# One-hot matrices stored tile by tile, with their 128 positions adjacent, in a transformer block with expert choice

## The chip, the cores and the metric

The kernel runs on one core of a Trainium2 chip. The metric is device time in microseconds of one launch. The core has TensorE (PE in the rows; its weight loads, which overlap matmuls, are PEld), VectorE (DVE), ScalarE (ACT), GpSimd (POOL) and SyncE (SP), which issues transfers. Each runs its own instructions in order and waits on semaphores for the others.

## The reference

x is 16 x 256 rows of 256 values, N = 4096 rows. First cross-attention, then a feed-forward layer in which each of 8 experts picks its 1024 best rows:

```
x = x + _L0_xattn_ref(_layernorm(x), ctx, ctx, Wq, bq, Wk, bk, Wv, bv)
x = x + _L0_ffn_ref(_layernorm(x), Wg, W1, b1, W2, b2)
# _L0_ffn_ref:
S = jax.nn.sigmoid(xt @ Wg).T            # 8 x 4096
G, I = jax.lax.top_k(S, k)               # k = 1024
ex = xt[I]
hid = jax.nn.gelu(einsum('ekh,ehf->ekf', ex, W1) + b1, approximate=False)
out = (einsum('ekf,efh->ekh', hid, W2) + b2) * G[..., None]
new_x = jnp.zeros_like(xt).at[I.reshape(-1)].add(out.reshape(-1, h))
```

## The kernel before

Rows are held as 32 tiles of 128 (NT = 32, P = 128), row t*128+p on partition p. The attention half (up to about 141 us) works through groups of four tiles. Products are made of 16-bit high and low parts, three matmuls for one (helper `pairs`, L1026). In its course the router's matmuls (L1120, four per tile: 128 weight columns from x2T, 16 moving columns from wg16) give the logits. A search on VectorE then finds each expert's threshold (to about 173 us), and two prefix products give each chosen row its place from 0 to 1023 in the expert's list; rows not chosen get a place out of reach. `split_places` cuts a place into loi (its low 7 bits, the position in a tile of the list) and hii (the tile of the list, 0 to 7).

The list of an expert is then made as a product. VectorE's `places(e)` copies the expert's column of loi to lo_e (L896, bf16) and of hii to hi_e, compares the latter with 0 to 7 (inhi) and writes val: for each tile t, inhi times the tile's number and inhi times the partition's number, 16 columns. `onehot` (L907), called four times (HOTS = 4), compares lo_e with the constants 0 to 127 in iota16, which GpSimd wrote once near the start (L407). The result oneh is 1 where row t*128+p has position k. TensorE's `list_of(e)` (L1257) adds up 32 matmuls, one per tile t, with oneh of that tile as weights (128 x 128) and val of that tile as the moving side (128 x 16). What comes out is the tile number and the partition number of the row at each place of the list. VectorE copies it out (idp, L915) and makes the row numbers (ids, L922); GpSimd gathers the rows with 8 indirect transfers (L447) into ex, SyncE turns them with DMA transposes (L287) into exT; for the first expert's first four tiles TensorE transposes (L1295) and ScalarE and VectorE (L1012) copy.

`expert(e)` on TensorE is 16 units of six matmuls with 512 columns (first layer; ScalarE applies gelu to each, L594 and L598, VectorE takes the low part, L967), then 8 tiles of 24 matmuls with 256 columns (second layer; VectorE L981, ScalarE L611, GpSimd scatters with addition, L460). Expert 0 is written out, experts 1 to 5 are a loop on every engine, 6 and 7 are written out. Lists are made ahead: list 0 before any expert, list 1 behind the first unit of expert 0 (SPLIT = 1), list e+2 behind the second layer of expert e. The one-hots of list e+2 are made by VectorE in the second layer of expert e, one call each in its tiles 3 to 6, `places` in its tile 0; those of lists 0 and 1 in one piece. The order on each engine is the order in which the code is written; semaphores named in `then_inc` and `wait_ge` join them: lo_s, val_s and hot_s (VectorE to TensorE), id_mm (back), const3 (the iota).

Of the kernel before, what the change touches and what calls it, by code (L numbers as in the profile page):

```python
# [26 lines left out]
BF16 = mybir.dt.bfloat16  # L27
# [5 lines left out]
P = 128  # L33


def build(nc, x_d, ctx_d, wq_d, bq_d, wk_d, bk_d, wv_d, bv_d, wg_d, w1_d, b1_d, w2_d, b2_d, out_d):
# [4 lines left out]
    NT = N // P  # L41
# [5 lines left out]
    KT = K // P  # L47
# [14 lines left out]
    HOTS = 4  # L62
# [6 lines left out]
    with ExitStack() as stack:  # L69
        def sb(name, shape, dt=F32):  # L70
            return stack.enter_context(nc.sbuf_tensor(name, shape, dt))

        def sem(name):
            return stack.enter_context(nc.semaphore(name))
# [9 lines left out]
        onesf = sb("onesf", [P, P])  # L84
        pick = sb("pick", [P, E])
        order16 = sb("order16", [P, 4, P], BF16)
        iota16 = sb("iota16", [P, P, NT], BF16)
        iota8 = sb("iota8", [P, NT, KT])
        tileno = sb("tileno", [P, NT, KT])
        partno = sb("partno", [P, 1])  # L90
# [61 lines left out]
        pos = sb("pos", [P, NT, E], I32)  # L152
        loi = sb("loi", [P, NT, E], I32); hii = sb("hii", [P, NT, E], I32)

        lo_e = sb("lo_e", [P, NT], BF16)
        hi_e = sb("hi_e", [P, NT])
        oneh = sb("oneh", [P, P, NT], BF16)
        inhi = sb("inhi", [P, NT, KT])
        val = sb("val", [P, NT, 2, KT], BF16)
        idp = sb("idp", [P, 2, KT])  # L160
# [44 lines left out]
        s = {n: sem(n) for n in names}  # L205
# [102 lines left out]
        def _(pool):  # L308
# [83 lines left out]
            def normed_rows(m):  # L392
# [6 lines left out]
                for t in range(TP):  # L399
# [4 lines left out]

            pool.wait_ge(s["const1"], 5)
            ln1_scale(0)
            pool.iota(iota16[:], [[1, P], [0, NT]], base=0, channel_multiplier=0,  # L407
                      allow_small_or_imprecise_dtypes=True).then_inc(s["const3"], 1)
            ln1_scale(1)
            pool.wait_ge(s["ld_bv"], 16)  # L410
# [216 lines left out]
        def _(dve):  # L627
# [264 lines left out]
            def places(e, first):  # L892

                if not first:
                    dve.wait_ge(s["id_mm"], e)
                dve.tensor_copy(lo_e[:], loi[:, :, bass.ds(e, 1)].rearrange("p t o -> p (t o)")).then_inc(s["lo_s"], 1)  # L896
                dve.tensor_copy(hi_e[:], hii[:, :, bass.ds(e, 1)].rearrange("p t o -> p (t o)")).then_inc(s["hie_s"], 1)
                dve.wait_ge(s["hie_s"], e + 1)
                dve.tensor_tensor(inhi[:], iota8[:], hi_e[:, :].unsqueeze(2).broadcast_to([P, NT, KT]), ALU.is_equal).then_inc(s["hi_s"], 1)
                dve.wait_ge(s["hi_s"], e + 1)  # L900
                dve.tensor_tensor(val[:, :, 0, :], inhi[:], tileno[:], ALU.mult).then_inc(s["val_s"], 1)
                dve.tensor_scalar(val[:, :, 1, :], inhi[:], partno[:, 0:1], None, ALU.mult).then_inc(s["val_s"], 1)
                dve.wait_ge(s["lo_s"], e + 1)

            def onehot(k0, k1):

                dve.tensor_tensor(oneh[:, k0:k1, :], iota16[:, k0:k1, :], lo_e[:, :].unsqueeze(1).broadcast_to([P, k1 - k0, NT]),  # L907
                                  ALU.is_equal).then_inc(s["hot_s"], 1)

            def read_list(e, first, from_=D_):  # L910
# [28 lines left out]
            def b1_of(e, first):  # L939
                if not first:  # L940
                    dve.wait_ge(s["h_hi"], 2 * FC * e)
                dve.tensor_copy(b1e[:], bcol[:, bass.ds(e * FC, FC)]).then_inc(s["b1e_s"], 1)
# [13 lines left out]
            def expert(e, first, next1, next2):  # L956


                b1_of(e, first)
                if not first and next1:  # L960
                    read_list(e + 1, False, D_)
                for u in range(2 * FC):
                    h, f = u // FC, u % FC
                    if first and u == SPLIT:
                        read_list(1, False, C_)
                    dve.wait_ge(s["h_hi"], 2 * FC * e + u + 1)
                    dve.tensor_tensor(hid[1][:, f, h * 512:(h + 1) * 512], g32[:, u % 2, :], hid[0][:, f, h * 512:(h + 1) * 512],  # L967
                                      ALU.subtract).then_inc(s["h_lo"], 1)
                    if u % 2 and u // 2 < 4:
                        w2_split(e, u // 2, first)  # L970
                    if u == KEEP:
                        keep(e, first)
                        if next1:
                            ids_of(e + 1, False)
                for t in range(KT):
                    dve.wait_ge(s["y_mm"], KT * e + t + 1)
                    if t == 0:
                        dve.wait_ge(s["b2e_s"], e + 1)
                    if not (first and t < 2):
                        dve.wait_ge(s["y_o"], KT * e + t - 1)  # L980
                    dve.scalar_tensor_tensor(yt[:, t % 2, :], C_[:, t % 2, 0:D], 1.0 / FS, b2e[:],  # L981
                                             ALU.mult, ALU.add).then_inc(s["y_t"], 1)
                    if next1 and t < 4:
                        w1_lo(e + 1, t)
                    if next2:
                        if t == 0:
                            places(e + 2, False)
                        elif t >= KT - 1 - HOTS:
                            if t < KT - 1:
                                j = t - (KT - 1 - HOTS)  # L990
                                onehot(P // HOTS * j, P // HOTS * (j + 1))

            def onehots():
                for j in range(HOTS):
                    onehot(P // HOTS * j, P // HOTS * (j + 1))

            dve.wait_ge(s["const2"], 5)
            places(0, True)
            dve.wait_ge(s["const3"], 1)
            onehots()  # L1000
# [20 lines left out]
        def _(pe):  # L1021
# [31 lines left out]
            for i in range(2):  # L1053
                for c in range(DC):
                    for e in range(DC):
                        last = pe.transpose(B_[:, i, e * D + c * P:e * D + (c + 1) * P], w_raw[:, i, c, e * P:(e + 1) * P], ident[:])
# [9 lines left out]
            for d in range(DC):  # L1066
                last = pairs(A_[:, 0, d * D:(d + 1) * D], lambda a, e: wkT[a][:, e, d * P:(d + 1) * P],
                             lambda b, e: wqcT[b][:, e, :], DC)
            last.then_inc(s["m_mm"], 1)
            pe.wait_ge(s["b_col"], 1)  # L1070
            for d in range(DC):
                for e in range(DC):
                    last = pe.matmul(A_[:, 1, P + d:P + d + 1], wqc[:, e, d * P:(d + 1) * P], bcol[:, NB1 + DC + e:NB1 + DC + e + 1],
                                     start=e == 0, stop=e == DC - 1)
# [145 lines left out]
            for h in range(2):  # L1220
                last = pe.transpose(A_[:, 0, h * P:(h + 1) * P], logit[:, h * HT:(h + 1) * HT, :].rearrange("p t e -> p (t e)"), ident[:])
# [28 lines left out]
            def list_of(e, first, to=D_):  # L1250

                pe.wait_ge(s["val_s"], 2 * (e + 1))
                if not first:
                    pe.wait_ge(s["id_ev"], e)
                pe.wait_ge(s["hot_s"], HOTS * (e + 1))
                for t in range(NT):
                    last = pe.matmul(to[:, 0, 0:2 * KT], oneh[:, :, t], val[:, t].rearrange("p a j -> p (a j)"),  # L1257
                                     start=t == 0, stop=t == NT - 1)
                last.then_inc(s["id_mm"], 1)

# [31 lines left out]
            for t in range(KT // 2):  # L1292
                pe.wait_ge(s[f"gat_{t}"], 16)
                for c in range(4):
                    last = pe.transpose(rowT16[t][:, c * P:(c + 1) * P], ex16[:, t, c * P:(c + 1) * P], ident16[:])  # L1295
# [27 lines left out]
```

## Time and profile before

| | us |
|---|---|
| median of 3 runs | 547.64 (547.56 to 548.38) |
| the profiled execution | 549.17 |
| its span, first to last instruction | 547.4 |
| TensorE busy | 491.1 (90%) |
| VectorE busy | 332.0 (61%) |
| ScalarE busy | 307.8 (56%) |
| GpSimd busy | 293.2 (54%) |
| mean granted TensorE clock, of its full speed | 0.944 |

The rows below have the time from the start of the span first, in us. "xN" counts instructions. A merged row's duration goes from its first start to its last end. What stands in brackets is idle time of the engine ahead of the row and what ended it. Busy time of TensorE is no measure of its use, since matmuls overlap: the distance of the starts is. PEclk is the granted clock as a share of 2.4 GHz; 0.50 is the level of 1.2 GHz.

### The profile page before, as it was taken

What the parts mean: (1) busy time and instruction counts of PE and PEld (TensorE: products, weight loads), DVE (VectorE), ACT (ScalarE), POOL (GpSimd) and SP (SyncE); (2) the same over time, 40 slices, a digit from 0 to 9 for tenths busy, and PEclk for the clock granted to TensorE, in tenths of its full rate; (3) what the DMA queues carried; (4) which work ended last, traced back from release to release, by engine and by line L of the source; (5) the groups of instructions that cost most, each with busy time, mean ns of one, the idle gap of its engine ahead of it and who ended that gap; (6) DMA issues with size and microseconds to landing.
All of it is one profiled execution on the core that took longest, in us unless ns stands there. A gap on an engine that the chain in (4) does not pass through costs nothing.

```text
span 547.4 us, 10408 instructions
## 1 busy us (share of the span) xinstructions
PE 491.1 (90%) x3671; PEld 351.6 (64%) x3671; DVE 332.0 (61%) x739; ACT 307.8 (56%) x562; POOL 293.2 (54%) x436
## 2 busy tenths in 40 slices
PE   4999999998523299999999999999999999999995
PEld 3777777777411245864874884794685586486484
DVE  7477777876588847547538538546645654733720
ACT  3666666654534059249439519727826925935921
POOL 5736998893600416734653671671672763555055
PEclk9999999998655589999999999999999999999998
DMA  7312555545195155943862771771782593484024
GB/s 237 107 46 69 153 147 134 137 131 150 38 275 157 41 130 172 171 72 127 141 121 76 156 144 27 200 149 19 195 162 29 152 180 55 136 126 49 0 31 50
DMA packets 91929, 64.19 MB, mean 117 GB/s; under 512 B 53044, under 2 KB 87800, under 8 KB 91896
## 3 DMA queue, kind: packets, MB, share of 16 engines
q1 hardware_dynamic: 79248, 46.42, 31.1%
q0 software_dynamic: 12288, 17.05, 18.8%
q8 instruction: 19, 0.31, 0.2%
q10 hardware_dynamic: 360, 0.30, 0.2%
q14 instruction: 14, 0.11, 0.1%
HBM read 35.83 MB, written 16.91 MB: 96 GB/s over the span
## 4 chain that ended last, share of the span: by engine, by line
PE 59%; issue 6%; DVE 5%; POOL 4%; DMA 2%; SPq 2%; ACT 1%; POOLq 0%; DVEq 0%; ACTq 0%
PE bank L1026 54%; PE bank L1257 3%; POOL out L460 2%; DVE junk L794 2%; SPq L266 2%; POOL xrow L387 1%; DMA out<-yo,ids_s 1%; DMA rows_d<-xrow 1%; POOL ex L447 1%; DVE thr L815 1%; PE bank L1233 1%; DMA ex<-rows_d,ids 1%; DMA yo<-xrow 0%; DVE oneh L907 0%; POOL xrow L379 0%
## 5 line engine op out<-in xcount | busy, mean ns | idle before, releaser
L1026 PE MATMUL bank<-w2h,xres 128*128 128x256 f16 x1024 | 169.0, 273 | 0.0
L1026 PE MATMUL bank<-exT,w1h 128*128 128x512 f16 x512 | 153.3, 381 | 0.6 <-DVE exT L1012 0.6
L1026 PE MATMUL bank<-w2l,xres 128*128 128x256 f16 x512 | 139.7, 273 | 0.0
L967 DVE TENSOR_TENSOR xres<-g,xres 128x512 f16<-128x512 f32 x128 | 87.6, 690 | 60.4 <-ACT xres L598 60.4
L460 POOL DMA_INDIRECT out<-yo,ids_s x64 | 101.0, 1577 | 25.6 <-issue 24.9
L1026 PEld LDWEIGHTS bank<-w2h,xres 128*128 128x128 f16 x1024 | 100.1, 98 | 12.5
L594 ACT ACTIVATE g<-bank,b1e 128x512 f32<-128x512 f32 x128 | 88.0, 688 | 25.4 <-PE bank L1026 20.3
L611 ACT ACTIVATE yo<-yt,ge 128x256 f32<-128x256 f32 x64 | 32.5, 508 | 119.5 <-DVE yt L981 119.5
L1026 PE MATMUL bank<-exT,w1l 128*128 128x512 f16 x256 | 97.7, 381 | 0.0
L1026 PEld LDWEIGHTS bank<-exT,w1h 128*128 128x128 f16 x512 | 49.8, 98 | 59.5 <-issue 1.4
L598 ACT ACTIVATE xres<-bank,b1e 128x512 f16<-128x512 f32 x128 | 87.2, 681 | 0.0
L981 DVE SCALAR_TENSOR_TENSOR yt<-bank,b2e 128x256 f32<-128x256 f32 x64 | 27.2, 425 | 88.6 <-PE bank L1026 87.9
L447 POOL DMA_INDIRECT ex<-rows_d,ids x64 | 65.4, 1021 | 19.6 <-issue 19.5
L445 POOL TENSOR_TENSOR pool_tick<-eps 128x1 f32<-128x1 f32 x8 | 4.7, 586 | 107.7 <-DVE ids L922 107.7
L1026 PEld LDWEIGHTS bank<-w2l,xres 128*128 128x128 f16 x512 | 50.0, 98 | 6.7
L459 POOL TENSOR_TENSOR pool_tick<-eps 128x1 f32<-128x1 f32 x64 | 15.4, 241 | 55.9 <-ACT yo L611 34.5
L1026 PEld LDWEIGHTS bank<-exT,w1l 128*128 128x128 f16 x256 | 25.1, 98 | 30.6 <-issue 0.6
L400 POOL TENSOR_SCALAR xn<-xres,st,rstd 128x256 f32<-128x256 f32 x24 | 29.0, 1219 | 0.6
L953 DVE SCALAR_TENSOR_TENSOR w2l<-w2r,w2h 128x512 f16<-128x512 f32 x32 | 22.1, 692 | 1.1
L371 POOL TENSOR_TENSOR xres<-xres,bv_bc 128x1024 f32<-128x1024 f32 x8 | 18.8, 2351 | 6.8 <-ACT xn L487 6.8
L643 DVE SCALAR_TENSOR_TENSOR w1l<-w1r,w1h 128x512 f16<-128x512 f32 x32 | 21.7, 682 | 0.0
L907 DVE TENSOR_TENSOR oneh<-iota,lo_e 128x1024 bf16<-128x1024 bf16 x32 | 21.4, 684 | 0.0
(215 smaller groups left out, 779.7 us busy)
## 6 DMA issues: line engine op xcount, KB each, us to landing
w1r<-in_L_ffn_W SPq DMA_DIRECT2D x8, 1024.0 KB, 6.6
w2r<-in_L_ffn_W SPq DMA_DIRECT2D x8, 1024.0 KB, 5.3
ctx<-in_ctx SPq DMA_DIRECT2D x8, 512.0 KB, 5.0
xres<-in_x SPq DMA_DIRECT2D x8, 512.0 KB, 5.9
rows_d<-xrow SPq DMA_DIRECT2D x8, 512.0 KB, 3.5
out<-xres SPq DMA_DIRECT2D x4, 1024.0 KB, 9.1
b_bc<-in_L_ffn_b SPq DMA_DIRECT2D x8, 128.0 KB, 4.5
ex<-rows_d,ids POOLq DMA_INDIRECT x64, 3.8
```

The costliest lines, as they stand in the source:

```text
L400: pool.tensor_scalar(xn2[:, m % 2, t], xres[:, m * TP + t], st2[:, t // 2, 1 + 3 * (t % 2):2 + 3 * (t % 2)], rstd2[:, t:t + 1], ALU.subtra ...
L447: pool.indirect_dma_start(out=ex[:, t, :], out_offset=None, in_=rows_d, in_offset=bass.IndirectOffsetOnAxis(ap=ids[:, t:t + 1], axis=0)).t ...
L460: pool.indirect_dma_start(out=rows_out, out_offset=bass.IndirectOffsetOnAxis(ap=ids_s[:, t:t + 1], axis=0), in_=yo[:, t, :], in_offset=Non ...
L594: act.activation(g32[:, u % 2, :], src, ACT.Gelu, bias=b1e[:, f:f + 1], scale=1.0 / (XS * FS))
L598: act.activation(hid[0][:, f, h * 512:(h + 1) * 512], src, ACT.Gelu, bias=b1e[:, f:f + 1], scale=1.0 / (XS * FS)).then_inc(s["h_hi"], 1)
L611: act.activation(yo[:, t, :], yt[:, t % 2, :], ACT.Copy, scale=ge[:, t:t + 1]).then_inc(s["y_o"], 1)
L643: dve.scalar_tensor_tensor(w1[1][:, c, cols], w1r[:, c, cols], FS, w1[0][:, c, cols], ALU.mult, ALU.subtract).then_inc(s["w1_lo_s"], 1)
L907: dve.tensor_tensor(oneh[:, k0:k1, :], iota16[:, k0:k1, :], lo_e[:, :].unsqueeze(1).broadcast_to([P, k1 - k0, NT]), ALU.is_equal).then_inc ...
L953: dve.scalar_tensor_tensor(w2[1][:, rows], w2r[:, rows], FS, w2[0][:, rows], ALU.mult, ALU.subtract).then_inc(s["w2_lo_s"], 1)
L967: dve.tensor_tensor(hid[1][:, f, h * 512:(h + 1) * 512], g32[:, u % 2, :], hid[0][:, f, h * 512:(h + 1) * 512], ALU.subtract).then_inc(s[" ...
L981: dve.scalar_tensor_tensor(yt[:, t % 2, :], C_[:, t % 2, 0:D], 1.0 / FS, b2e[:], ALU.mult, ALU.add).then_inc(s["y_t"], 1)
L1026: last = pe.matmul(out, lhs(a, c), rhs(b, c), start=i == 0, stop=i == len(terms) - 1)
```

## The change

oneh is stored as [partition, tile, position] and no more as [partition, position, tile], so that one tile's 128 weight columns are adjacent, where they were 32 elements apart. A call of `onehot` makes all 128 positions of 8 tiles and no longer 32 positions of all 32 tiles; it writes one run of 1024 elements. For that iota16 shrinks from 128 x 32 to 128 elements per partition and is read once per tile. lo_e holds each row's position twice, side by side, and is read in pairs, 64 times over for a tile.

```
-        iota16 = sb("iota16", [P, P, NT], BF16)
+        iota16 = sb("iota16", [P, P], BF16)
-        lo_e = sb("lo_e", [P, NT], BF16)
+        lo_e = sb("lo_e", [P, NT, 2], BF16)
-        oneh = sb("oneh", [P, P, NT], BF16)
+        oneh = sb("oneh", [P, NT, P], BF16)
...
-            pool.iota(iota16[:], [[1, P], [0, NT]], base=0, channel_multiplier=0,
+            pool.iota(iota16[:], [[1, P]], base=0, channel_multiplier=0,
...
-                dve.tensor_copy(lo_e[:], loi[:, :, bass.ds(e, 1)].rearrange("p t o -> p (t o)")).then_inc(s["lo_s"], 1)
+                dve.tensor_copy(lo_e[:], loi[:, :, bass.ds(e, 1)].broadcast_to([P, NT, 2])).then_inc(s["lo_s"], 1)
...
-            def onehot(k0, k1):
-
-                dve.tensor_tensor(oneh[:, k0:k1, :], iota16[:, k0:k1, :], lo_e[:, :].unsqueeze(1).broadcast_to([P, k1 - k0, NT]),
+            def onehot(j):
+
+                part = slice(NT // HOTS * j, NT // HOTS * (j + 1))
+                dve.tensor_tensor(oneh[:, part].rearrange("p t (k o) -> p t k o", o=2),
+                                  iota16[:].rearrange("p (k o) -> p k o", o=2).unsqueeze(1).broadcast_to([P, NT // HOTS, P // 2, 2]),
+                                  lo_e[:, part].unsqueeze(2).broadcast_to([P, NT // HOTS, P // 2, 2]),
                                   ALU.is_equal).then_inc(s["hot_s"], 1)
...
-                                onehot(P // HOTS * j, P // HOTS * (j + 1))
+                                onehot(j)
...
-                    last = pe.matmul(to[:, 0, 0:2 * KT], oneh[:, :, t], val[:, t].rearrange("p a j -> p (a j)"),
+                    last = pe.matmul(to[:, 0, 0:2 * KT], oneh[:, t], val[:, t].rearrange("p a j -> p (a j)"),
```

Every engine has the same number of instructions in the same order as before, and the same waits. VectorE's sequence ahead of the first list, with the tiles of the words above, shows the one size that differs there:

```order
 L884 TENSOR_SCALAR hii<-pos 128x32
-L896 CAST lo_e<-loi 128x32
+L896 CAST lo_e<-loi 128x64
 L897 CAST hi_e<-hii 128x32
 L899 TENSOR_TENSOR inhi<-iota,hi_e 128x256
 L901 TENSOR_TENSOR val<-inhi,tileno 128x32x8
 L902 TENSOR_SCALAR val<-inhi,partno 128x32x8
```

Nothing moved there; the cast writes twice as many elements.

## Rows read from the trace of the kernel before

**Rows 1.** Page, part 4: shares of the chain that ended last, by line

```profile
PE bank L1026 54%; PE bank L1257 3%; POOL out L460 2%; DVE junk L794 2%; SPq L266 2%; POOL xrow L387 1%; DMA out<-yo,ids_s 1%; DMA rows_d<-xrow 1%; POOL ex L447 1%; DVE thr L815 1%; PE bank L1233 1%; DMA ex<-rows_d,ids 1%; DMA yo<-xrow 0%; DVE oneh L907 0%; POOL xrow L379 0%
```

**Rows 2.** Chain in order of time, the experts: start, duration (us), work

```profile
237.77 1.93 PE bank L1257 x32
239.71 41.70 PE bank L1026 x288
...
455.92 1.78 PE bank L1257 x32
```

**Rows 3.** Instructions in order of time around list 0

```profile
180.79 2.02 PE L1257 MATMUL bank<-val,oneh 128*128 128x16 bf16 x32 [5.02 <-DVE oneh L907]
182.85 0.17 DVE L915 COPY idp<-bank 128x16 f32<-128x16 f32 x1 [0.40 <-PE bank L1257]
```

**Rows 4.** Weight loads of both kinds; min/median/max ns; L1120 in order of time

```profile
L1257 PEld LDWEIGHTS bank<-val,oneh x256: 137/167/191, 180.8 to 457.4; 128*128 128x128 bf16 x128
L1120 PEld LDWEIGHTS bank<-wg,yo x96: 94/96/100, 63.3 to 134.1; 128*128 128x128 f16 x96
133.73 0.56 PE L1120 MATMUL bank<-wg,yo 128*128 128x16 f16 x16 [0.81 <-DMA yo<-xrow]
134.14 0.27 PE L1026 MATMUL bank<-vh,pTh 128*128 128x256 f16 x1
```

**Rows 5.** L1257 in stretches: length, PE busy, PEld busy, PEclk, DMA share, GB/s

```profile
180.00:184.00 4.00, 2.02 (x32) 1.95 (x32) 0.50 0.01 4
...
455.00:459.00 4.00, 1.94 (x32) 1.96 (x32) 1.00 0.50 62
```

**Rows 6.** TensorE around list 1, in order of time; a stretch with PEclk (0.57)

```profile
194.90 0.63 PE L1026 MATMUL bank<-exT,w1l 128*128 128x512 f16 x1
195.32 2.05 PE L1257 MATMUL bank<-val,oneh 128*128 128x16 bf16 x32
197.23 0.59 PE L1026 MATMUL bank<-exT,w1h 128*128 128x512 f16 x2
...
197.66 0.38 PE L1026 MATMUL bank<-exT,w1l 128*128 128x512 f16 x1
...
195.50:196.00 0.50, 0.50 (x13) 0.50 (x11) 0.00 (x0) 0.35 (x1) 0.00 (x0) 0.57 0.58 194
```

**Rows 7.** Instructions in order of time ahead of expert 0

```profile
186.95 2.53 DVE L907 TENSOR_TENSOR oneh<-iota,lo_e 128x1024 bf16<-128x1024 bf16 x4
...
192.24 0.42 DVE L1012 COPY exT<-bank 128x512 f16<-128x512 f16 x1 [2.43 <-PE bank L1295]
```

**Rows 8.** VectorE's groups: shapes, count, busy us, mean ns of one, idle before

```profile
L907 DVE TENSOR_TENSOR oneh<-iota,lo_e 128x1024 bf16<-128x1024 bf16 x32 | 21.4, 684 | 0.0
L635 DVE TENSOR_TENSOR vl<-bank,vh 128x1024 f16<-128x1024 f32 x7 | 8.6, 1225 | 11.0 <-ACT vh L507 11.0
L635 DVE TENSOR_TENSOR vl<-bank,vh 128x512 f16<-128x512 f32 x2 | 1.3, 687 | 0.0
```

**Rows 9.** VectorE at a turn of the loop, in order of time

```profile
412.29 0.42 DVE L981 SCALAR_TENSOR_TENSOR yt<-bank,b2e 128x256 f32<-128x256 f32 x1 [1.60 <-PE bank L1026]
412.87 0.17 DVE L942 COPY b1e<-bcol 128x8 f32 x1 [0.15 <-issue]
```

**Rows 10.** GpSimd and ScalarE near the start, in order of time

```profile
14.45 4.18 POOL L407 IOTA iota<- 128x4096 bf16 x1
...
23.94 2.06 ACT L487 ACTIVATE xn<-xres,nmr,rstd 128x256 f32<-128x256 f32 x4
```

**Rows 11.** ScalarE in the last first layer, catching up after a wait

```profile
511.30 0.69 ACT L594 ACTIVATE g<-bank,b1e 128x512 f32<-128x512 f32 x1 [0.24 <-DVE xres L967]
...
512.45 0.69 ACT L594 ACTIVATE g<-bank,b1e 128x512 f32<-128x512 f32 x1
```

**Rows 12.** SyncE's four transposes for expert 0, and TensorE, in order of time

```profile
196.54 5.13 SPq L287 DMA_TRANSPOSE exT<-ex  x4
...
206.29 0.60 PE L1026 MATMUL bank<-exT,w1h 128*128 128x512 f16 x2
```

More of the change, by code:

```diff
@@ L990, in expert @@
                                 j = t - (KT - 1 - HOTS)
-                                onehot(P // HOTS * j, P // HOTS * (j + 1))
+                                onehot(j)
             def onehots():
                 for j in range(HOTS):
-                    onehot(P // HOTS * j, P // HOTS * (j + 1))
+                    onehot(j)
             dve.wait_ge(s["const2"], 5)
```

## Prediction

> **What bounds the kernel now.** I read the shares of the chain that ended last first. Matmuls of the helper at L1026 hold 54% of it, and the 256 list matmuls of L1257 3% [rows 1]. Then the chain in order of time [rows 2]: lists and expert matmuls take turns back to back, 237.77 + 1.93 is where the 41.70 us of expert matmuls begin, and the same again up to the last list at 455.92 and the expert matmuls behind it. So TensorE's own sequence sets the expert half, and a list stands bare in it: nothing runs on TensorE beside it. The first list (180.79) is also bare, but for another reason: TensorE had waited for the one-hots, and VectorE waits for its end [rows 3], GpSimd's gathers behind it.
>
> What does a list matmul take? It has 128 weight columns and 16 moving columns, as a router matmul at L1120 has [rows 4]. Their weight loads last 167 and 96 ns. Durations overlap, so the pace counts. Sixteen router matmuls start at 133.73 and the next work starts at 134.14: 0.41 us, 25.6 ns each [rows 4]. The list of 237.77 takes 1.93 us on the chain, 60 ns each, the fastest, of 455.92, 1.78, 56 ns [rows 2]. Between the two kinds three things differ: the router reads each weight column next to the last one and in f16, in groups of four; the list steps 32 elements (64 bytes) from one weight column to the next, in bf16, in one group of 32. The step is what the change removes. That it is the step is supported by the first list: TensorE's clock was granted at 0.50 there, its 1.2 GHz level, and its 2.02 us, less some 0.2 for the last one, over 31 still give 59 ns, the pace of the full clock [rows 3, 5]. A column or issue limit of TensorE itself would have doubled, as a 512-column matmul does: one from 194.90 to 195.32, 0.42 us, before the clock rose, two from 197.23 to 197.66, 0.215 each, after [rows 6]. A limit outside of TensorE's clock, the reading of the weights, does not.
>
> **The change, part by part.**
>
> *Six lists at the full clock (237.8 to 455.9).* Now 11.43 us together, the first 1.93 and the last 1.78 [rows 2]. At the router's pace 32 matmuls take 32 x 0.0256 = 0.82 us, six of them 4.9. Gain **6.5 us**. The bound from below is a pace that holds for 16 only, from above nothing better than 25.6 is in the trace.
>
> *The first list, at half clock.* No contiguous run of small matmuls stands in the trace at 1.2 GHz. Bounds: the pace is not TensorE's (25.6 ns, 31 x 0.0256 + 0.2 = 0.99 us, gain 1.0) or it is and doubles (51 ns, 1.78 us, gain 0.25). I take the second, since everything else on TensorE doubled [rows 6].
>
> *The second list.* It starts at 195.32 at half clock; the 195.5 to 196 slice has a mean of 0.57, so the clock rose near 195.93, while TensorE was at work [rows 6]. It now takes 195.32 to 197.23 = 1.91. After, it starts 0.22 earlier, 195.10; until 195.93 16 matmuls pass at 51 ns, the other 16 take 0.41: 1.24 us, gain 0.67; with 25.6 ns all through 0.82, gain 1.1.
>
> *The one-hots on VectorE.* Four operations of 1024 elements before and after. Now 684 ns each for 1024 bf16 elements, where 1024 elements at L635 take 1225 ns and 512 take 687: two elements per cycle [rows 8]. The new form reads lo_e in runs of two (its double), iota16 in rows of 128 and writes one run of 1024. No row has runs of two. Bounds: 684 ns (no cost), or 1225 ns, one per cycle, +0.54 each. I take 684, because the innermost pair is adjacent in all three tensors, which is all that the operation had of lo_e's pairs before. The cover, if not: in the expert loop VectorE idles 1.60 us ahead of a tile of the second layer [rows 9], enough for 0.54; before the second list the one-hots end at 189.48 and the exT copy that releases TensorE waits to 192.24, 2.76 us later, enough for 4 x 0.54 = 2.2 [rows 7]. Before the first list there is none: they end where TensorE's 5.02 us of waiting ends [rows 3], +2.2 us.
> A rule of the Trainium skill bears on this (Vector Engine (DVE) Microarchitecture Reference, section 5.1, Performance modes): two results per cycle need 16-bit types, an innermost step of 1 and more than one element innermost, and rows of two were measured to keep the mode. By that rule the cost is 0, as I took it; no run here shows a row of two yet.
>
> *lo_e.* One cast of 64 in place of 32 elements; L635's slope is (1225 - 687)/512 = 1.05 ns per element [rows 8], so +0.03 us. It is bare once, before the first list [rows 3]; in the loop it lies in VectorE's idle time, and before the second list in the 2.76 us.
>
> *iota16 on GpSimd.* The 4.18 us of L407 (14.45 to 18.63) shrink by a factor of up to 32. Behind it on GpSimd stand the scale of the second four tiles and add_bv. ScalarE takes the scale up at 23.94, 5.3 us behind the iota and with no idle time ahead of that row, so it wasn't what it waited for [rows 10]. Gain at the end: 0, and that GpSimd is earlier by 4 us there delays nothing.
>
> *What a shorter list uncovers.* ScalarE needs 511.30 to 512.45 = 1.15 us for a unit when it catches up, TensorE 1.295 (6 matmuls), so ScalarE doesn't become the bound [rows 11]. The second half of the first expert's rows is turned by four transposes, the last issue ending at 201.67; TensorE reads them from 206.29 [rows 12]. That is 4.6 us, less a flight that no row shows here; the second list eats 0.7 to 1.1 of it; gathers and transposes move with the first list. Each later expert's gather starts from ids made inside the expert, so all of it moves together. At a turn of the loop TensorE's sequencer has the list's time to pass the branch: 1.9 us now, 0.8 then. VectorE's own turn costs at most from 412.29 to 412.87, 0.58 us [rows 9], so I cost it at nothing.
>
> **Sum.** 6.5 + 0.25 + 0.67 - 0.03 = 7.4 us. Against its own execution, 549.17 us with a span of 547.4, that is 541.8 and 540.0. The median of the runs, 547.64, lies 1.5 below that execution; the forecast is 547.64 - 7.4 = **540.2 us**. With the half-clock pace at 25.6 ns the sum is 6.5 + 1.0 + 1.1 = 8.6: 539.0.
>
> **The rivals.**
> *The pace does not last.* Rows show it for 16 in a row only, behind long matmuls that let instructions pile up. If matmuls 17 to 32 go at 57 ns, each full-clock list loses 16 x 0.031 = 0.5 us, six 3.1: 543.3. If instead the branch takes more than 0.8 us, four turns lose up to 1.1 each, 4.4: 544.6. Against: no gap behind any list now, and VectorE's 0.58.
> *One-hots at one element per cycle:* -2.2 of the gain: 542.4.
> *The clock rises later.* TensorE worked from 192.6 or so, when the exT copy had ended, to 195.93, 3.3 us, at half clock [rows 6, 7]; as much again would cost half of it, 1.6: 541.8. Against: the dense work starts earlier and stays as dense.
> *The step isn't it.* The pace stays 56 to 61 ns, from bf16 or the long group: 547.6. Against: the half-clock list above, and that groups of four on the same columns run at 25 ns with no break between them.
> The Trainium skill has a rule on this side (TensorE: Matmul & The Clock Gate, Weight-path perf modes): fast weight load reads 128 columns of a non-FP32 type, packed or strided, up to a step of 1,024 elements. By it a step of 32 is loaded fast already and the time stays 547.6; the 167 against 96 ns speak against it.
> *Slower:* the one-hot costs more than one cycle per element for its runs of two. Its place is VectorE before both lists. An extra x on each costs 4x at the first and, past the cover, 4x - 2.76 at the second; 8x - 2.76 exceeds 7.4 from x = 1.27 us, an operation of 1.95. At two cycles per element (2 x 1.07 + 0.15 = 2.29, x = 1.6) it is 10.0 - 7.4 = 2.6 slower: 550.2. The longest 1024 elements of two sources on VectorE in my rows take 1225 ns [rows 8].
>
> **How the numbers follow.** Forecast 0.70; pace doesn't last 0.10; one-hots at one per cycle 0.07; clock later 0.03; step isn't it 0.06; slower 0.04. The range takes the forecast's two ends, 539.0 and 540.2, with 0.2 for the spread of runs, and goes up over 541.8 and 542.4 to 543.3: 538.8 to 543.4, about 0.85. What a measurement can tell from no change is about 0.2%, 1.1 us. Faster by more: 0.70 + 0.10 + 0.07 + 0.03 = 0.90; within: 0.06; slower: 0.04.
>
> **What would show it.** List matmuls at a pace near 25 ns and weight loads near 96; stretches between expert matmuls of 0.8 us in place of 1.9; the first list's duration tells 25 from 50 ns at half clock; one-hots at 684 ns; no idle time of TensorE at the turns; the half-clock stretch ending at 195.9 or so; the iota at 0.2 us with nothing else moved by it. Wrong would be: a list at 1.9 us, an idle TensorE behind a list, or exT transposes waited for at the second half of the first expert.

## The result, and the profile after

| | before | after |
|---|---|---|
| median of the runs on the same chip, us | 548.01 (547.56 to 549.37, 4 runs) | 540.66 (539.06 to 541.63, 4 runs) |
| the profiled execution, us | 549.17 | 540.94 |
| its span, us | 547.4 | 539.2 |
| mean granted TensorE clock | 0.944 | 0.943 |

The ratio is 0.9859, with a 95% interval of 0.9828 to 0.9889. On a second chip it was 0.9848 (0.9833 to 0.9863), with 539.85 us. Forecast were 540.2 us and a range of 538.8 to 543.4.

The page of the kernel after, its parts 1 and 4. PE is busy for 483.1 us, 491.1 before. In part 4 the list matmuls are L1260 now, the expert matmuls L1029:

```profile
span 539.2 us, 10408 instructions
...
PE 483.1 (90%) x3671; PEld 343.1 (64%) x3671; DVE 331.4 (61%) x739; ACT 308.2 (57%) x562; POOL 290.6 (54%) x436
...
PE bank L1029 55%; POOL out L460 2%; DVE junk L794 2%; SPq L266 2%; PE bank L1260 1%; POOL xrow L387 1%; DMA out<-yo,ids_s 1%; DMA rows_d<-xrow 1%; POOL ex L447 1%; DVE thr L815 1%; PE bank L1236 1%; DMA ex<-rows_d,ids 1%; DMA yo<-xrow 0%; DVE oneh L908 0%; POOL xrow L379 0%
```

The lists' share of the chain went from 3% [rows 1] to 1%, and nothing else rose by more than a point. The chain of waits in order of time, after (start, duration, work):

```profile
235.29 0.79 PE bank L1260 x32
236.08 41.70 PE bank L1029 x288
277.78 0.79 PE bank L1260 x32
278.57 0.12 issue
278.69 41.85 PE bank L1029 x288
320.54 0.79 PE bank L1260 x32
```

Against [rows 2]: a list holds 0.79 us where it held 1.93, and the 288 expert matmuls behind it hold 41.70 as before. What is new is the 0.12 of "issue" (time in which the engine waited for nothing that the profile shows) and 41.85 in place of 41.70 where a turn of the loop lies: that is looked at below. The instructions behind these rows, by the tile oneh (min/median/max ns, first and last start) and by line and shape (busy us, mean ns, idle before):

```profile
L1260 PEld LDWEIGHTS bank<-val,oneh x256: 95/96/151, 179.7 to 449.3; 128*128 128x128 bf16 x128
...
L908 DVE TENSOR_TENSOR oneh<-iota,lo_e 128x1024 bf16<-128x1024 bf16 x32 | 21.4, 684 | 0.0
```

A weight load lasts 96 ns, the router's number [rows 4], where it lasted 167; a one-hot still 684 ns [rows 8].

Where the 8.2 us between the two profiled spans lie, from the starts of matched instructions in the two traces:

| stretch | before | after | difference | forecast |
|---|---|---|---|---|
| start of the span to list 0's first matmul | 180.79 | 179.72 | 1.07 | -0.03 |
| list 0's first matmul to expert 0's first | 12.02 | 11.48 | 0.54 | 0.25 |
| expert 0's first matmul to the one behind list 1 | 4.42 | 3.41 | 1.01 | 0.67 |
| from there to list 2 | 40.38 | 40.51 | -0.13 | 0 |
| list 2 to the end of the span | 309.8 | 304.1 | 5.74 | 6.5 |

Without the first row this is 7.16 us, against a forecast of 7.4. Of the 5.74, the six lists from their start to the next expert matmul give 5.71: 11.55 us before, 5.84 after.

These are distances in one execution of each kernel. In the profiled execution of the same changed kernel on the second chip the last four differences are 0.49, 1.01, -0.85 and 5.73, together 6.4: there TensorE's clock rose 5.2 us behind expert 0's first matmul, and in the execution of the table 3.7 behind.

### The profile page after: what moved, and what is told of

Read it like the earlier page. It is cut to its first block, busy times and chain, and to the rows that moved or that the text cites. A ratio compares the mean times of both kernels' runs of the same rounds, so it can differ in the third digit from the quotient of the medians.

```text
span 539.2 us, 10408 instructions
## 1 busy us (share of the span) xinstructions
PE 483.1 (90%) x3671; PEld 343.1 (64%) x3671; DVE 331.4 (61%) x739; ACT 308.2 (57%) x562; POOL 290.6 (54%) x436
## 4 chain that ended last, share of the span: by engine, by line
PE 58%; issue 6%; DVE 6%; POOL 5%; DMA 2%; SPq 2%; ACT 1%; POOLq 0%; DVEq 0%; ACTq 0%
PE bank L1029 55%; POOL out L460 2%; DVE junk L794 2%; SPq L266 2%; PE bank L1260 1%; POOL xrow L387 1%; DMA out<-yo,ids_s 1%; DMA rows_d<-xrow 1%; POOL ex L447 1%; DVE thr L815 1%; PE bank L1236 1%; DMA ex<-rows_d,ids 1%; DMA yo<-xrow 0%; DVE oneh L908 0%; POOL xrow L379 0%
## 5 line engine op out<-in xcount | busy, mean ns | idle before, releaser
L1029 PE MATMUL bank<-w2h,xres 128*128 128x256 f16 x1024 | 169.0, 273 | 0.0
L1029 PE MATMUL bank<-exT,w1h 128*128 128x512 f16 x512 | 153.3, 381 | 1.0 <-issue 0.6
L1029 PE MATMUL bank<-w2l,xres 128*128 128x256 f16 x512 | 139.6, 273 | 0.0
L970 DVE TENSOR_TENSOR xres<-g,xres 128x512 f16<-128x512 f32 x128 | 87.7, 690 | 60.5 <-ACT xres L598 52.1
L1029 PEld LDWEIGHTS bank<-w2h,xres 128*128 128x128 f16 x1024 | 100.2, 98 | 12.5
L1029 PE MATMUL bank<-exT,w1l 128*128 128x512 f16 x256 | 97.5, 381 | 0.0
L1029 PEld LDWEIGHTS bank<-exT,w1h 128*128 128x128 f16 x512 | 49.6, 98 | 60.2 <-issue 2.2
L445 POOL TENSOR_TENSOR pool_tick<-eps 128x1 f32<-128x1 f32 x8 | 4.7, 587 | 100.6 <-DVE ids L925 100.6
L1029 PEld LDWEIGHTS bank<-w2l,xres 128*128 128x128 f16 x512 | 50.1, 98 | 6.6
L459 POOL TENSOR_TENSOR pool_tick<-eps 128x1 f32<-128x1 f32 x64 | 18.8, 293 | 57.4 <-ACT yo L611 36.1
L1029 PEld LDWEIGHTS bank<-exT,w1l 128*128 128x128 f16 x256 | 25.1, 98 | 30.7 <-issue 0.8
```

Source lines behind the costliest of these rows:

```text
L1029: last = pe.matmul(out, lhs(a, c), rhs(b, c), start=i == 0, stop=i == len(terms) - 1)
```

## The experiments

### One step at a time: 2, 4, 8, 16 elements

The forecast blamed the step of 32 elements between weight columns. A rival would be anything else that the new layout changed with it: which addresses the one-hots are written to, or rows of lo_e's doubles. Four kernels use a layout between the two: G tiles are interleaved, so the step is G elements. iota16 then holds each constant G times and lo_e each position once. A call makes all positions of eight tiles, as in the changed kernel, and for G = 16 half of the positions of 16 tiles. For G = 2, against the changed kernel:

```
-oneh = sb("oneh", [P, NT, P], BF16)
+oneh = sb("oneh", [P, NT // G, P, G], BF16)
...
-pe.matmul(..., oneh[:, t], val[:, t], ...)
+pe.matmul(..., oneh[:, t // G, :, t % G], val[:, t], ...)
```

> The one-hots of two tiles are interleaved: weight columns lie 2 elements (4 bytes) apart; iota16 holds each constant twice, lo_e each position once. All else as in the changed kernel. If any gap between weight columns makes the load slow, lists at the full clock go at 56 to 61 ns a matmul (1.9 us each) and the time is some 7 us above the changed kernel's, 547 to 548 us. If what counts is how many columns a 16-byte stretch of memory holds (four here), they stay at 25 ns (0.8 us) and the time at 539 to 542 us. One-hots 684 ns under both.

> The one-hots of four tiles interleaved: weight columns 4 elements (8 bytes) apart. If any gap makes the load slow: 56 to 61 ns a matmul at the full clock. If the columns in a 16-byte stretch count (two here): still 25 ns, lists of 0.8 us. A price that grows with the step would give something between, some 30 to 40 ns, with the 4-byte step below it.

> The one-hots of eight tiles interleaved: weight columns 8 elements (16 bytes) apart. If columns in a 16-byte stretch count (one here): 56 ns a matmul or more, as with 64 bytes, lists of 1.8 us or more, 546 to 548 us. If the price grows with the step up to 64 bytes: between 25 and 56 ns.

> The one-hots of sixteen tiles interleaved: weight columns 16 elements (32 bytes) apart, a call of the one-hots makes 64 positions of 16 tiles. If columns in a 16-byte stretch count, the same pace as with 16 and 64 bytes, 56 to 61 ns. If the price grows with the step, less than at 64 bytes.

Measured, one run each, beside 548.33 for the kernel before on that chip (the times of the steps 1 and 32 are the medians of the result above):

| step | bytes | time, us | list matmul pace at full clock, ns | at half clock, ns |
|---|---|---|---|---|
| 1 (after) | 2 | 540.66 | 25.4 | 26.6 |
| 2 | 4 | 539.01 | 25.4 | 26.8 |
| 4 | 8 | 540.63 | 33.2 | 33.0 |
| 8 | 16 | 547.11 | 59.5 | 60.5 |
| 16 | 32 | 548.14 | 61.2 | 61.7 |
| 32 (before) | 64 | 548.01 | 55.9 to 61.9 | 58.1 |

The times of single runs differ by some 3 us for reasons at the start of the span (below), and where the clock rises in expert 0 moves them too: with steps of 8 and 16 it was 7.3 and 8.0 us behind expert 0's first matmul, and from that matmul to expert 1's first it took 48.14 and 48.51 us against 46.75 in the kernel before. The pace of the lists varies far less. It is the distance from the list's first to its last matmul start over 31. The step of 2 elements: its weight loads by line and shape (busy us, mean ns, idle before), and a list in the chain of waits:

```profile
L1261 PEld LDWEIGHTS bank<-val,oneh 128*128 128x128 bf16 x256 | 7.8, 99 | 6.3 <-issue 6.1
```
```profile
275.82 0.79 PE bank L1261 x32
```

The same two views of the step of 4:

```profile
L1261 PEld LDWEIGHTS bank<-val,oneh 128*128 128x128 bf16 x256 | 9.7, 117 | 6.2 <-issue 6.1
```
```profile
276.66 1.04 PE bank L1261 x32
```

and of the step of 8, which stands as in the kernel before [rows 2, 4]:

```profile
L1261 PEld LDWEIGHTS bank<-val,oneh 128*128 128x128 bf16 x256 | 16.5, 168 | 6.2 <-issue 6.1
```
```profile
279.44 1.90 PE bank L1261 x32
```

So the step is the cause. The one-hots take 683 to 685 ns in all four, and all four have bf16 weights in one group of 32 matmuls, the two other things in which the lists differed from the router. The price goes from nothing at 4 bytes, over 8 ns a matmul at 8 bytes, to 34 ns at 16 bytes and 36 at 32; 64 bytes cost about the same (30 to 37). The Trainium skill (Advanced Engine Details and Errata, SBUF Cachelines) has lines of 16 bytes and says that a line needs at least two hits to absorb the memory's latency. That the full price begins at 16 bytes, one element per line, agrees. That a step of 8 bytes would be free by it, with its two elements per line, does not: 33.2 against 25.4 ns. And the rule of the Trainium skill that the forecast weighed as a rival (TensorE: Matmul & The Clock Gate, Weight-path perf modes: strides up to 1,024 elements are loaded fast) is against these rows if it is read as a speed: at a step of 8 elements a load lasts 168 ns, at one or two 98 to 99 (means). Why the reading slows, no run here shows.

### The position stored once

> lo_e holds each position once and the one-hot reads it with an innermost step of 0 (one element 128 times), the rest as in the changed kernel. If the adjacent pair is what keeps two elements per cycle, the one-hots take about 1225 ns in place of 684; the four before the first list are bare, +2.2 us, the others lie in idle time: 542.5 to 543 us. If the engine keeps its rate with one repeated element, 684 ns and the changed kernel's 540.7 us.

```
-lo_e = sb("lo_e", [P, NT, 2], BF16)
+lo_e = sb("lo_e", [P, NT], BF16)
...
-lo_e[:, part].unsqueeze(2).broadcast_to([P, NT // HOTS, P // 2, 2])
+lo_e[:, part].unsqueeze(2).broadcast_to([P, NT // HOTS, P])
```

Measured: 543.31 us (541.93 to 544.05, 6 runs), ratio 0.9922 (0.9895 to 0.9949). By the ratios some 3.5 to 4 us of the change's gain are gone. The one-hots by line and shape, the ones ahead of list 0 in the chain of waits, and those ahead of expert 0 in order of time with GpSimd's gathers beside them:

```profile
L908 DVE TENSOR_TENSOR oneh<-iota,lo_e 128x1024 bf16<-128x1024 bf16 x32 | 38.4, 1216 | 0.0
```
```profile
175.31 4.54 DVE oneh L908 x4
```
```profile
185.68 4.62 DVE L908 TENSOR_TENSOR oneh<-iota,lo_e 128x1024 bf16<-128x1024 bf16 x4
...
185.76 1.96 POOL L447 DMA_INDIRECT ex<-rows_d,ids  x1 [0.30 <-issue]
...
188.02 1.97 POOL L447 DMA_INDIRECT ex<-rows_d,ids  x1 [0.30 <-issue]
...
190.29 0.94 POOL L447 DMA_INDIRECT ex<-rows_d,ids  x1 [0.30 <-issue]
```

The same two places in the kernel after, in the chain and in order of time:

```profile
177.16 2.41 DVE oneh L908 x4
```
```profile
185.41 2.54 DVE L908 TENSOR_TENSOR oneh<-iota,lo_e 128x1024 bf16<-128x1024 bf16 x4
...
185.48 1.43 POOL L447 DMA_INDIRECT ex<-rows_d,ids  x1 [0.30 <-issue]
...
187.22 0.95 POOL L447 DMA_INDIRECT ex<-rows_d,ids  x1 [0.30 <-issue]
```

A one-hot without the pair takes 1216 ns, the pace that the prediction calls one element per cycle; the double of lo_e is what keeps 684. The group ahead of the first list is bare, 4.54 against 2.41, +2.13 us. The group ahead of the second was to be hidden by 2.76 us of cover, and it was not: from list 0's first matmul to expert 0's first it is 13.02 us here (180.00 to 193.02) and 11.48 after, 1.54 more. The one-hots themselves are in time. What is late is GpSimd: two of its gathers stand beside them, and these took 1.96 and 1.97 us where they took 1.43 and 0.95 (+0.53 and +1.02, together the 1.55). VectorE's longer operations go together with the longer gathers, and the exT transposes wait for the gathered rows. Behind that the kernels are alike: from expert 0's first matmul to expert 1's it is 45.12 us here, 44.73 and 45.45 in the two executions of the change. The Trainium skill has a rule for such a hold (SBUF — State Buffer, SBUF: two separate sides): a port pair shared by VectorE and GpSimd is taken for a whole instruction by whichever starts first, on VectorE also by operations with two inputs in SBUF, against a GpSimd operation that reads SBUF. The sizes fit a gather that waits for less than one one-hot: 0.48 us more than 0.95, of a one-hot's 0.68; 1.01 and 1.02 more, of 1.22. But the gather of 187.22 above started 0.01 us behind a one-hot and took 0.95. So the mechanism is argued, not shown; that the gathers are slower with the longer one-hots is shown.

### The list ahead of the last tile: what the pause at a turn is

The four lists at loop turns (list 3 to list 6) have a pause behind them that did not stand there before. TensorE in order of time, after, at a turn:

```profile
277.50 0.97 PEld L1260 LDWEIGHTS bank<-val,oneh 128*128 128x128 bf16 x32
277.61 0.96 PE L1260 MATMUL bank<-val,oneh 128*128 128x16 bf16 x32
...
278.69 0.11 PEld L1029 LDWEIGHTS bank<-exT,w1h 128*128 128x128 f16 x2 [0.21 <-issue]
278.69 0.60 PE L1029 MATMUL bank<-exT,w1h 128*128 128x512 f16 x2
```

and at the last list, where no turn follows:

```profile
448.58 0.95 PE L1260 MATMUL bank<-val,oneh 128*128 128x16 bf16 x32
...
449.39 0.59 PE L1029 MATMUL bank<-exT,w1h 128*128 128x512 f16 x2
```

From the list's start to the next expert matmul it is 1.08 us at the turn (277.61 to 278.69), 0.81 without (448.58 to 449.39). The profile shows no semaphore that TensorE waited for. What is left is its own sequencer at the turn, the branch or the first instructions behind it. If that is so, work of more length than a list ahead of the turn hides it. Edit: list e+2 goes ahead of the last tile of the second layer, so that 24 matmuls of 256 columns stand between it and the turn. For that VectorE's one-hots move from tiles 3 to 6 to tiles 2 to 5.

```
 # TensorE, second layer of expert e
+                    if next2 and t == KT - 1:
+                        list_of(e + 2, False)
...
-                if next2:
-                    list_of(e + 2, False)
 # VectorE, second layer
+                elif t >= KT - 2 - HOTS:
+                    if t < KT - 2:
+                        j = t - (KT - 2 - HOTS)
```

> TensorE makes the list of expert e+2 ahead of the last tile of the second layer and no more behind it, VectorE its one-hots one tile earlier (tiles 2 to 5). In the changed kernel's trace TensorE pauses 0.26 to 0.29 us behind the list at each of the four turns of the loop, where 0.025 is its pace. If that is the branch, no longer covered by a list of 0.8 us, 24 matmuls of 109 ns (2.6 us) cover it now: no pause at the turns, 4 x 0.24 = 1.0 us less, some 539.7 us. If the pause comes with the step from small to large matmuls or with the list's own end, it moves to behind the list, and the time stays at 540.7 us.

Measured: 538.2 us (538.01 to 538.73, 4 runs), ratio 0.9834 (0.9796 to 0.9871). The chain of waits:

```profile
273.24 0.79 PE bank L1260 x32
274.03 41.70 PE bank L1029 x288
315.72 0.79 PE bank L1260 x32
```

The "issue" is gone, and the period is 42.48 us (273.24 to 315.72) against 42.76 after (277.78 to 320.54). Over the four turns the periods add up to 1.0 us less. By the ratios the time is lower by 0.8 to 1.4 us, which agrees, but the interval alone would not show it. The periods show that the turn was it: the list is followed by large matmuls here too, 0.025 us behind its last one, so neither the list's end nor the change of size makes the pause.

The same move in the kernel before, with its old layout:

> The kernel before (one-hots 64 bytes apart) with only the list moved ahead of the last tile of the second layer. If the pause at the turns of the changed kernel is the branch that a list of 1.9 us had covered, there is nothing to win here: no pause before or after, the time that of the kernel before. If moving the list helped in another way, 1 us less here too.

Measured: 547.85 us (545.51 to 549.16, 10 runs), ratio 1.0003 (0.9984 to 1.0021). Its chain of waits:

```profile
276.92 1.89 PE bank L1257 x32
278.81 41.70 PE bank L1026 x288
320.51 1.96 PE bank L1257 x32
```

Nothing to win: a list of 1.9 us covered the turn. The kernel with a step of 4 elements lies between. From the start of a list's last matmul to the next expert matmul it is 0.12 to 0.18 us at its turns (0.03 elsewhere), and 0.26 to 0.32 with the steps 1 and 2 (0.025 elsewhere). The shorter the last work ahead of the turn, the more of the turn shows. What the sequencer does in that time is not in the profile.

### The first list: read it first

List 0 runs at half clock. Its duration went from 2.02 us [rows 3] to 1.00, but of this 1.0 only 0.54 arrived at expert 0's first matmul. In order of time, after:

```profile
179.49 1.89 DVE L643 SCALAR_TENSOR_TENSOR w1l<-w1r,w1h 128x512 f16<-128x512 f32 x3
...
179.72 1.00 PE L1260 MATMUL bank<-val,oneh 128*128 128x16 bf16 x32 [5.03 <-DVE oneh L908]
...
181.30 0.17 DVE L918 COPY idp<-bank 128x16 f32<-128x16 f32 x1
```

The list ends at 180.72, and its result is read at 181.30, with no idle time ahead of the copy: VectorE makes three pieces of w1's low part between the one-hots and the copy. Before, the list of 2.02 us outlasted them and the copy waited 0.40 us for it [rows 3]. Edit: all four pieces go behind the copy.

```
-                for j in range(3):
-                    w1_lo(0, j)
                 read_list(0, True)
                 ids_of(0, True)
-                w1_lo(0, 3)
+                for j in range(4):
+                    w1_lo(0, j)
```

> VectorE copies list 0 out and makes its row numbers ahead of the four low parts of the first expert's weights, three of which stood ahead of that before. In the changed kernel's trace list 0 ends near 180.72 but VectorE reads it at 181.30, behind those three. If VectorE's order holds it back: from the last one-hot's start to the first matmul of expert 0 some 0.55 us less than in the changed kernel; the low parts then lie beside the gathers. If the gathers wait for something else, nothing changes.

Measured, one run: 537.88 us, span 536.1. In order of time:

```profile
177.82 1.00 PE L1259 MATMUL bank<-val,oneh 128*128 128x16 bf16 x32 [5.03 <-DVE oneh L908]
...
178.86 0.17 DVE L918 COPY idp<-bank 128x16 f32<-128x16 f32 x1 [1.18 <-PE bank L1259]
...
184.39 1.07 POOL L447 DMA_INDIRECT ex<-rows_d,ids  x1 [0.30 <-issue]
...
188.50 1.01 PE L1028 MATMUL bank<-exT,w1h 128*128 128x512 f16 x2 [0.61 <-issue]
```

The copy stands 1.04 us behind the list's start where it stood 1.58 behind, and expert 0's first matmul 10.68 us behind it where it was 11.48: 0.80 less, of which 0.54 is the copy's and the rest the gathers': the first four took 4.32 us together in place of 4.60, the third 0.95 and not 1.43, since the one-hots stand later now; the fourth, beside them, 1.07 and not 0.95. The clock rose at 190.78 here, 2.3 us behind expert 0's first matmul, and the second list ran at full clock. The single time can't be read as a gain of 2.8, for that reason and for the one that the next experiment gives.

### Is the small iota worth anything

The forecast gave the shrunken iota nothing. The old one, 4.18 us, is written again in addition, into a tensor that nobody reads:

```
+iotaw = sb("iotaw", [P, P, NT], BF16)
...
+            pool.iota(iotaw[:], [[1, P], [0, NT]], base=0, channel_multiplier=0, ...)
             pool.iota(iota16[:], [[1, P]], base=0, channel_multiplier=0, ...)
```

> The old constant of 128x4096 is written once more, into a tensor that nothing reads, in the place where it was, ahead of the new one on GpSimd; the rest as in the changed kernel. If those 4.2 us were hidden, the time stays at 540.7 us and ScalarE's second group of four normalized tiles starts without idle time ahead of it. If taking them away was a part of the gain (the changed kernel's trace has everything before the first list 1.1 us earlier), the time rises to some 541.7 us and ScalarE waits for GpSimd there.

Measured: 541.2 us (539.7 to 542.13, 4 runs), ratio 0.988 (0.9838 to 0.9922), not to be told from the 0.9859 and 0.9848 of the change; an effect of 1 us could not be told from these intervals. What the order of time shows is more:

```profile
13.95 4.18 POOL L408 IOTA iotaw<- 128x4096 bf16 x1
...
23.19 2.06 ACT L490 ACTIVATE xn<-xres,nmr,rstd 128x256 f32<-128x256 f32 x4
```

As in the kernel before [rows 10], ScalarE takes up what GpSimd made behind it with no idle time. So nothing points to the iota for the 1.07 us of the table's first row. They are within what the start varies by. The one-hots of list 0 began at 178.16, 177.08 and 177.53 us in the profiled executions of the kernel before, of the one after and of this one. They began between 174.65 and 175.66 in the ten others, the kernel with the old layout and the list moved ahead among them (174.71). The stretch from 14 to 16 us shows two kinds. The columns are the length, the busy time and count of PE, PEld, DVE, ACT and POOL, the granted clock, the DMA share and GB/s, for after:

```profile
14.00:16.00 2.00, 2.00 (x11) 1.50 (x11) 1.79 (x4) 1.95 (x4) 0.21 (x2) 1.00 0.49 163
```

and the same for the same kernel in an execution on another chip:

```profile
14.00:16.00 2.00, 2.00 (x21) 1.81 (x21) 1.93 (x4) 1.96 (x4) 0.19 (x2) 1.00 0.81 269
```

11 matmuls stand in it in one execution, 21 in the other of the same code. The second has list 0 at 178.05, 1.67 us earlier. The clock's column says 1.00 in both because the records of the clock begin only with its first rise, at 17.41 and at 13.83 us. The pace tells the two levels apart: the 256-column matmuls start 0.21 us apart in the first, 0.11 in the second. The rise was at 18.43, 17.41 and 18.04 us in the three late executions and at 12.3 to 13.8 in the ten others. What sets it these runs don't tell. That is why a single run is read here by the distances inside it, and not by its time.

### All of it together

The list ahead of the last tile, the list read first, and one step more: list matmuls wait only for the one-hots of their own eight tiles, which the new layout allows and the old did not (a call made 32 positions of all tiles).

```
-            pe.wait_ge(s["hot_s"], HOTS * (e + 1))
             for t in range(NT):
+                if t % (NT // HOTS) == 0:
+                    pe.wait_ge(s["hot_s"], HOTS * e + t // (NT // HOTS) + 1)
```

> The changed kernel with three more things: the list ahead of the last tile of the second layer, list 0 read and its row numbers made ahead of the four low parts, and the list's matmuls waiting for the one-hots of their own eight tiles only, which the new layout allows. The turns give 1.0 us as in e6_list_ahead. Reading first gave 0.5 to 0.6 on VectorE's side. The split waits let 24 of list 0's matmuls run beside the one-hots: it ends about 0.4 us behind the last one-hot and no more 1.2, some 0.65 us. Together 2.2 us less than the changed kernel on the same chip. If GpSimd's gathers are slowed by VectorE's low parts that now stand beside them (a gather took 1.43 and 1.96 us beside one-hots, 0.95 alone), the first two gains shrink to 0.3 or nothing, and 1.3 remains.

> The changed kernel once more, on the same chip as e9_all and e10_old_ahead: the same trace but for the granted clock near the start (it rose between 12.3 and 18.4 us in the runs so far); some 7 us below the kernel before.

Measured on one chip: 536.8 us (535.57 to 539.01, 5 runs), ratio to the kernel before 0.9798 (0.9772 to 0.9823); the change alone 539.85 (539.8 to 540.09, 4 runs). That is 3.05 us less, where 2.2 were expected. The first list, in order of time:

```profile
175.50 2.49 DVE L908 TENSOR_TENSOR oneh<-iota,lo_e 128x1024 bf16<-128x1024 bf16 x4
...
176.33 0.36 PE L1260 MATMUL bank<-val,oneh 128*128 128x16 bf16 x8 [3.23 <-DVE oneh L908]
...
178.04 0.39 PE L1260 MATMUL bank<-val,oneh 128*128 128x16 bf16 x8 [0.22 <-DVE oneh L908]
...
178.47 0.17 DVE L918 COPY idp<-bank 128x16 f32<-128x16 f32 x1 [0.48 <-PE bank L1260]
```

Three quarters of the list pass beside the one-hots. Against the profiled execution of the change on the same chip, whose one-hots began at 175.42: from the one-hots' start to expert 0's first matmul it is 12.68 us (175.50 to 188.18) and not 14.16, 1.48 less. The periods of the chain are 42.48 as in the list-ahead kernel, 1.0 us over the four turns. Together that is 2.5. The rest is the clock's: it rose 2.8 us behind expert 0's first matmul here and 5.2 there, and from expert 0's first to expert 1's first it took 44.57 us against 45.45, 0.9 less. Against the first execution of the change (44.73) it would be 0.2, so this part is not to be counted on.

## Why the prediction was right, and where its terms were off

*What bounds the kernel.* Right: the lists stood bare in TensorE's sequence, and what they lost the chain lost, with 41.70 us behind them unchanged but for the turns.

*The step is the cause.* Right, and now shown by the four steps rather than argued from the router. One of the two signs that the prediction read was weaker than it took it to be. From 59 ns at half clock it argued that a limit of TensorE's columns or issue would have doubled there. With a step of 8 or more the pace is 56 to 62 ns at either clock, but the adjacent columns keep their pace too, 26.6 against 25.4. So not doubling did not single out the reading of the weights; the comparison with the router did the work.

*Six lists, 6.5 us.* The list itself came out as said, 0.79 us, at 25.4 ns for all 32. The mis-sized part is the turn: the rival "the pace does not last" had the branch as its second form, priced at up to 1.1 each, and it came true in a small size, 0.23 to 0.27 at each of four turns, about 1.0 us. With it came one of the prediction's own signs of being wrong, an idle TensorE behind a list. The prediction saw where it would be and took nothing for it, since VectorE's own turn seemed short [rows 9]; VectorE's turn says nothing on how much queued work TensorE's needs. 6.5 less 1.0 is the rest of the 5.74, with 0.04 a list to the good.

*List 0, 0.25 us.* The term's step that failed: "it is and doubles" (51 ns). The pace at half clock is 26.6 ns, so it is not TensorE's columns that set it there either; the other bound, 1.0 us on TensorE, was the right one. That the path gained 0.54 and not 1.0 is a second miss, of the other sign: what is late next is VectorE with its three w1 pieces, which the prediction had not priced. They were in the trace, 2.02 us of list with only 0.40 us of waiting behind them [rows 3].

*List 1, 0.67 us.* It lay wholly in half clock and went at 28 ns in the mean (its first step is 73 ns, the others 27), a gain of 1.01 us; the bound named for this case was 1.1. The clock rose at 194.90, behind this list, and 3.7 us behind expert 0's first matmul; before it was 195.93 and 3.1. The stretch up to just behind the rise, after, the columns as above:

```profile
194.00:195.00 1.00, 1.00 (x31) 0.76 (x28) 0.00 (x0) 0.96 (x2) 0.00 (x0) 0.55 0.31 101
```

So some 512-column matmuls behind the list, which had the full clock before, ran at half: 194.61 to 195.17 are two at 0.28 in the mean, and that is in the table's -0.13. The rival "the clock rises later" is in this form 0.13 us, and 0.85 in the second execution of the same kernel, where the rise came 5.2 us behind expert 0's first matmul. Over the kernels it came 2.3 us behind (the list read first) to 8.0 us (step 16), and 7.7 with the old layout and the list moved. So it is not the same in every execution, the 3.1 of the kernel before is no fixed value of the old layout either, and what sets it these runs don't tell.

*One-hots at 684 ns.* Right. The page that the prediction names for it (the Trainium skill, Vector Engine (DVE) Microarchitecture Reference, section 5.1) has measured two elements per partition; that many rows of two keep the rate is what the 684 ns here show. But the cover named for them, 2.76 us ahead of expert 0, was wrong as a mechanism: the kernel with the single position lost 1.54 there, through GpSimd. Had one-hots come out at one element per cycle, the loss would have been 2.13 + 1.54 = 3.7 and the rival's time 543.9 rather than 542.4, past the end of the range (543.4). The 543.31 us measured are nearer to this than to 542.4. They lie 3.9 below the kernel before on that chip, where the change lies 7.4 to 8.1 below it.

*lo_e and the iota.* Right: the cast ahead of list 0 is 0.20 us where it was 0.19, and nothing waits for the iota's 4 us in the order of time.

*The whole.* 7.4 was forecast, 7.16 shown without the noise of the start, but from terms that erred both ways: +0.29 and +0.34 at the half-clock lists, -0.76 and -0.13 behind them. The agreement within 0.3 us is better than its parts, and partly luck: in the second execution the same four stretches give 6.4. The medians of the runs differ by 7.4 and, on the second chip, 8.1 us.

## What to carry to other kernels

Weights for many small matmuls should be laid out so that neighbouring columns are within 4 bytes of each other; from 16 bytes on a matmul of 128 bf16 weight columns and 16 moving columns costs 56 to 62 ns here and not 25, at either clock. When a bare stretch on the bounding engine shrinks, look at everything that it used to cover: here a loop turn of its own sequencer and three operations of another engine, which together ate 1.5 us, and which moving two steps gave back. And a longer operation on VectorE is not hidden by VectorE's idle time alone, if GpSimd works beside it on the path.

## What the runs showed of the hardware that was not expected

Small matmuls (128 weight columns, 16 moving) go at 26.6 ns at half clock and 25.4 at full, while 512-column ones double, 0.42 and 0.215 us [rows 6]. A step of 8 bytes between weight columns costs something already, 33 ns a matmul, and 4 bytes nothing. An indirect gather holds GpSimd for 0.95 us in most cases (the first two of an expert take up to 1.42 beside other work of VectorE), for up to 1.43 beside one-hots of 0.68 us, and for 1.96 beside one-hots of 1.22 us. From the last small matmul to the next large one a loop turn shows as 0.26 to 0.32 us in place of 0.025 behind 0.8 us of small matmuls, and as nothing behind 1.9.
